# The norm's factor moved behind the rotation, in the first attention stage of a Perceiver block

## The reference

```python
def _rms_norm(t, w):                       # per head of 32 words
    var = jnp.mean(t * t, axis=-1, keepdims=True)
    return t * jax.lax.rsqrt(var + EPS) * w
def _rope(q, k, cos, sin):
    q1, q2 = jnp.split(q, 2, axis=-1); k1, k2 = jnp.split(k, 2, axis=-1)
    q_out = jnp.concatenate([q1 * cos - q2 * sin, q2 * cos + q1 * sin], axis=-1)
    k_out = jnp.concatenate([k1 * cos - k2 * sin, k2 * cos + k1 * sin], axis=-1)
    return (q_out, k_out)
q = _rms_norm(q, q_norm_w); k = _rms_norm(k, k_norm_w)
q, k = _rope(q, k, cos, sin)
attn = jnp.einsum('bhqd,bhkd->bhqk', q, k) * scale      # causal, softmax, times v, projection
```

## Time and profile before

| | us |
|---|---|
| Median of 3 runs (lowest, highest) | 2095.78 (2095.14, 2098.06) |
| The profiled execution: its own time | 2095.99 |
| Its span in the trace | 2094.4 |
| TensorE matmuls busy | 1946.4 (93%) |
| VectorE, ScalarE, GpSimd busy | 695.6, 542.0, 195.7 |
| The chain that ended last | TensorE 69%, issue 19%, GpSimd 4%, VectorE 4% |

### The profile page before, as it was taken

The page is one execution under the profiler, slowest core; times in us unless marked ns, Lnnn a source line. Parts: engine busy times, 40 slices in busy tenths (PEclk is TensorE's granted clock), DMA queues, the critical chain, the costliest instruction groups (busy, mean ns, idle before and its releaser), DMA issues.

```text
span 2094.4 us, 37583 instructions
## 1 busy us (share of the span) xinstructions
PE 1946.4 (93%) x15760; PEld 996.3 (48%) x15760; DVE 695.6 (33%) x1500; ACT 542.0 (26%) x1113; POOL 195.7 (9%) x182
## 2 busy tenths in 40 slices
PE   5888887999999999999997999999999999999976
PEld 2444464333333333333334656575666666565543
DVE  2666651122111211112122433334433333333322
ACT  1333211222222222222111233232323333232320
POOL 1122203000000000000003000000000000000000
PEclk8899998999999999999998999999999999999987
DMA  9544136999999999999975030000000100000000
GB/s 344 210 161 161 60 128 259 391 396 390 378 391 377 380 361 380 377 378 378 364 285 176 22 105 18 27 21 27 21 17 21 26 22 21 27 11 26 11 1 10
DMA packets 86296, 374.96 MB, mean 179 GB/s; under 512 B 7782, under 2 KB 25702, under 8 KB 53432
## 3 DMA queue, kind: packets, MB, share of 16 engines
q1 hardware_dynamic: 79544, 355.71, 44.5%
q0 software_dynamic: 6656, 17.77, 2.4%
HBM read 357.73 MB, written 16.45 MB: 179 GB/s over the span
## 4 chain that ended last, share of the span: by engine, by line
PE 69%; issue 19%; POOL 4%; DVE 4%; ACT 2%; DMA 1%; SPq 1%; another core or an unknown queue 0%; POOLq 0%; DVEq 0%; ACTq 0%
PE ps L1284 25%; PE ps L1462 16%; PE ps L1444 16%; POOL arena L540 4%; PE ps L1669 2%; PE ps L1452 2%; PE ps L1470 1%; DMA arena<-in_wproj0T 1%; PE ps L1590 1%; ACT arena L718 1%; PE ps L1344 1%; PE ps L1433 1%; PE ps L1374 1%; PE ps L1549 1%; PE ps L1611 1%
## 5 line engine op out<-in xcount | busy, mean ns | idle before, releaser
L1284 PE MATMUL ps<-arena 128*128 128x512 f32 (+3 forms) x3208 | 909.1, 440 | 26.1 <-ACT arena L661 8.5
L1284 PEld LDWEIGHTS ps<-arena 128*128 128x128 f32 x3208 | 548.0, 194 | 353.0 <-issue 291.2
L1462 PE MATMUL ps<-arena 128*32 128x512 f32 x3072 | 373.6, 594 | 0.0
L1444 PE MATMUL ps<-arena 128*32 128x512 f32 x3072 | 363.9, 596 | 0.7 <-issue 0.6
L540 POOL TENSOR_TENSOR arena<-arena 128x1 f32<-128x1 f32 (+3 forms) x80 | 128.3, 1604 | 1111.5 <-DVE arena L898 635.9
L1082 DVE COPY arena<-ps 128x512 f32<-128x512 f32 x96 | 66.4, 692 | 482.6 <-PE ps L1462 482.6
L1444 PEld LDWEIGHTS ps<-arena 128*32 128x32 f32 x3072 | 109.2, 109 | 226.0 <-issue 226.0
L1462 PEld LDWEIGHTS ps<-arena 128*32 128x32 f32 x3072 | 100.3, 109 | 198.2 <-issue 195.7
L768 ACT ACTIVATE arena<-ps 128x512 f32<-128x512 f32 x96 | 57.3, 597 | 353.0 <-PE ps L1444 353.0
L1181 DVE TENSOR_REDUCE arena<-ps 128x1 f32<-128x257 f32 x128 | 54.2, 424 | 154.7 <-PE ps L1549 152.6
L798 ACT ACTIVATE arena<-ps,arena 128x257 f32<-128x257 f32 x128 | 60.7, 477 | 141.4 <-PE ps L1284 141.4
(11 more groups left out here) (194 smaller groups left out, 1313.2 us busy)
## 6 DMA issues: line engine op xcount, KB each, us to landing
arena<-in_w SPq DMA_DIRECT2D x64, 4096.0 KB, 13.8
arena<-in_ctxT SPq DMA_DIRECT2D x8, 2056.0 KB, 7.9
arena<-in_ctxT SPq DMA_DIRECT2D x32, 514.0 KB, 3.7
arena<-in_ctx SPq DMA_DIRECT2D x8, 2048.0 KB
xe_rows<-arena SPq DMA_DIRECT2D x8, 616.0 KB
arena<-in_b POOLq DMA_DIRECT2D x32, 154.0 KB, 7.5
arena<-xe_rows SPq DMA_DIRECT2D x32, 154.0 KB
y_rows<-arena POOLq DMA_DIRECT2D x32, 154.0 KB, 6.2
```

The lines of the kernel that those rows point to most:

```text
L1284: ins = pe.matmul(dst, lhsT, rhs, start=(n == 0), stop=(n == len(pairs) - 1))
L1444: ins = pe.matmul(ps[q4[n], t, :], xeT[s][:, k, q4[t]], w1_sb[s][:, k, n * D:(n + 1) * D], start=(k == 0), stop=(k == KD - 1))
L1462: ins = pe.matmul(ps[q4[n], ST + t, :], hT[s][:, t, c, q4[n]], w2_sb[s][:, n * HB + c, :], start=(c == 0), stop=(c == HB - 1))
```

## The change

Before, the first of the five operations multiplies queries and keys (banks 4 and 5) by the factor `rs` and puts the result into SBUF (`qkn`); three multiplies by cosines and sines read it there, and an add gives `qkr`. After, the three multiplies read banks 4 and 5 directly, the add goes to `qkn`, VectorE waits for the factor only there, and a last operation multiplies `qkn` by it into `qkr`. The number and the sizes of the operations stay.

```diff
-                dve.wait_ge(rs_rdy, i + 1)
-                my.step(TT(qkn, ps[:, 4:6, :].rearrange("p a (h d) -> p (a h) d", h=H),
-                           bc(rs.unsqueeze(2), P, 2 * H, DH), ALU.mult))
                 v4 = "p (a h) d -> p a h d"
-                qn4, A4, B4 = (a.rearrange(v4, a=2) for a in (qkn, ropeA, ropeB))
+                A4, B4 = (a.rearrange(v4, a=2) for a in (ropeA, ropeB))
+                qn4 = ps[:, 4:6, :].rearrange("p a (h d) -> p a h d", h=H)
                 my.step(TT(A4, qn4, bc(CW.unsqueeze(2), P, 2, H, DH), ALU.mult))
                 hd = DH // 2
                 my.step(TT(B4[:, :, :, 0:hd], qn4[:, :, :, hd:DH],
                            bc(SW[:, :, 0:hd].unsqueeze(2), P, 2, H, hd), ALU.mult))
                 my.step(TT(B4[:, :, :, hd:DH], qn4[:, :, :, 0:hd],
                            bc(SW[:, :, hd:DH].unsqueeze(2), P, 2, H, hd), ALU.mult))
-                TT(qkr, ropeA, ropeB, ALU.add).then_inc(qkr_rdy, 1)
+                my.step(TT(qkn, ropeA, ropeB, ALU.add))
+                dve.wait_ge(rs_rdy, i + 1)
+                TT(qkr, qkn, bc(rs.unsqueeze(2), P, 2 * H, DH), ALU.mult).then_inc(qkr_rdy, 1)
```

## The result

| | before | after |
|---|---|---|
| Median of 10 runs, us (lowest, highest) | 2097.18 (2095.14, 2098.83) | 2091.61 (2087.61, 2092.11) |
| The profiled execution: its own time; its span | 2095.99; 2094.4 | 2089.46; 2087.9 |

The ratio is 0.9971 with a 95% interval of 0.9961 to 0.9981: 5.6 us faster, clear of noise. All of it arises in the first stage: from the issue of the first expert's weights (296.8 us before, 290.5 after) to the end it is 1797.6 and 1797.4 us.

A forecast was written before the change was run, and what follows sets the result against it. TensorE, busy for 93% of the span, was taken as the bound. Round 1 losing 0.5 us, rounds 2 to 6 gaining 0.5, round 7 1.8 and the clock 0.8 gave -2.6: 2093.4, as median 2093.2, range 2089.0 to 2097.2.

The forecast's parts named there:

- the likelier case: Whole kernel: a time within about 0.2%, 4.2 us, of no change, chance 0.67; faster 0.27, slower 0.06.
- The change on VectorE: Rotation out of PSUM: operations take 1.23 us, half ones 0.69; in round 2 VectorE is done 2.55 us earlier.
- Middle rounds: Rounds 2 to 6: line 1367 starts 0.1 us sooner in each, 0.5 us gained in all (0 to 0.9).
- Round 0 and round 1: Round 0 gains 3.6 to 7.1 us, all hidden by round 1's context transfer with its own date; 0.5 us lost.
- Round 7: Line 1367 no longer waits for VectorE: 1.8 us gained, 4.0 if the projection ran warm.
- The clock in the middle rounds: Falls of the clock after the idle stretch cost 1.6 us each; half a fall fewer, 0.8 us gained.
- Rival (a): Luck of the clock: two or more falls fewer, 2090.8 us, down to 2087.6 with none left; chance 0.21.
- The shared port: Rounds 0, 1, 7: the add might stand until the root's end, 259.8 in round 7; the sum stays.
- Rival (d): Rotation and root slow each other until they run one behind the other: 2095.5 us; chance 0.08.
- rival (b): Round 0's gain comes through if round 1's loads don't hold it: 3.6 to 7.1 us more, 2086 to 2090; chance 0.06.
- Rival (c): Slower: round 1 cold from line 1328 through line 1344 and the projection, rounds 2 and 5 fall too: 2100.5 us; 0.06.
- The signs: Trace of after: last of five operations waits for root, line 1367 never for VectorE, round 1's line 1344 at 77.4 or later.

The follow-up runs named there:

- e3: New order in round 0 alone, old order in the other rounds, against the kernel before: 2095.43 us, ratio 0.9994.
- e6: Changed kernel with the clearing of the experts' rows moved behind tile 2's context loads: 2085.56 us, ratio 0.9945 to the kernel before.
- e4: The whole change run again, beside the same runs of the kernel before as the partial ones: 2091.08 us, ratio 0.9969.
- e1: New order in round 7 alone, old order in rounds 0 to 6, against the kernel before: 2094.1 beside 2096.99 us, ratio 0.9987.
- e12: Kernel before (old order) with ten idle transposes a round and the clearing moved behind tile 2's context loads: 2084.68 us, ratio 0.9943.
- e11: Changed kernel with ten idle transposes a round and the clearing moved behind tile 2's context loads: 2077.94 us, ratio 0.9909 to the kernel before.
- e10: Kernel before (old order) with ten idle transposes behind line 1367 in each round: 2086.93 beside 2097.36 us, ratio 0.9953.
- e7: Changed kernel with ten idle transposes ahead of line 1374's wait in each round: 2081.79 us beside 2097.46 for the kernel before, ratio 0.993.
- e2: New order in rounds 2 to 6 alone, old order elsewhere, against the kernel before: 2094.59 us, ratio 0.9986.
- e5: Kernel before (old order) with the clearing of the experts' rows moved behind tile 2's context loads: 2096.35 beside 2097.46 us, ratio 0.9996.
- e8: Kernel before (old order) with GpSimd making the 128x32 root twice in each round: 2146.92 us beside 2096.11.
- e9: Changed kernel with GpSimd making the root twice in each round: 2116.55 us, beside 2096.11 for the kernel before.

## Why the prediction was right, point by point

The forecast was 2093.2 and the measured median 2091.6, inside the range. Part of this closeness is luck: the forecast starts from the first median of before, 2095.78, and over ten runs that is 2097.18. The gain is 5.6 us where 2.6 were forecast. I had held a time within 0.2% for the likelier case, and it is 0.29%, faster. The reasons, in the order of the prediction:

**The change on VectorE** was right: 1.22 and 0.69 us for the operations out of PSUM, in runs of 16 words too; the last multiply 2.7 us ahead of line 1367 in round 2.

**Middle rounds**: the place was right, the size half. I took 0.1 us for a round, from the first matmul of line 1367. It is 0.2 us, just outside my bounds (0.9 for five rounds; 1.0 came). What I had left out is that all its weight loads now run ahead. The first four transposes, for which ScalarE waits, take 0.45 us in the chain that ended last, where they took 0.61 to 0.65 before.

**Round 0 and round 1**: round 0's 3.64 us came (3.8). The further gain by a clock that holds did not: line 1374 of round 0 still took 1.94 us. That the transfer takes the gain back in round 1 was right in kind (e3, e6); line 1344 at 78.09 lies within what I had worked out, and the cold line 1328 took 3.35 us, a little over my 3.23. What failed is the step that gave the transfer a fixed date, and with it the sentence that all of round 0 is hidden: in e4 line 1344 started at 75.19, which I had named as a sign of being wrong. The transfer landed at 72.4 in one trace of the changed kernel and at 69.8 in the next. In the three traces with the old order in round 0 and the old place of the clearing, line 1367 of round 1 starts at 84.57, 85.40 and 86.01; in the three with the new one at 84.49, 81.58 and 85.54. That is 1.5 us earlier on the mean, with 0.6 us of it from an earlier start-up, so I put the term at about 1 us gained instead of 0.5 lost, and three traces a side can't size it better than to a microsecond.

**Round 7**: 1.8 us forecast, 1.9 in e1, 2.1 between e12 and e11. The 4.0 us that I had named for a warm projection came too, in the kernels with the filling; first e10, then e7:

```profile
248.25 5.40 PE L1284 MATMUL ps<-arena 128*128 128x512 f32 x8 [0.71 <-ACT arena L729]
...
256.73 1.09 PE L1367 MATMUL ps<-arena 128*128 128x128 f32 x8 [3.08 <-DVE arena L953]
```

```profile
248.86 3.71 PE L1284 MATMUL ps<-arena 128*128 128x512 f32 x8 [0.71 <-ACT arena L729]
...
253.44 1.09 PE L1367 MATMUL ps<-arena 128*128 128x128 f32 x8 [0.87 <-DVE arena L953]
```

With the projection at 3.71 us the last multiply is late next, and line 1367 comes 24.60 us behind that of round 6, where it is 28.57 in e10: 4.0 us. What I missed stands behind round 7. From line 1367 of round 7 to the weights' issue it is 34.2 us in all four unfilled traces with the old order there (before, e2, e3, e5) and 32.7 in all four with the new one (after, e1, e4, e6). The windows of that stretch show why; first before, then after, columns as in the earlier trace rows:

```profile
266.20:271.44 5.24, 2.69 (x37) 1.91 (x37) 2.72 (x4) 1.23 (x2) 0.00 (x0) 0.53 0.01 2
271.44:282.15 10.71, 10.71 (x44) 9.03 (x48) 4.32 (x11) 0.39 (x1) 0.00 (x0) 0.75 0.01 2
```

```profile
261.39:266.09 4.70, 1.67 (x37) 1.24 (x37) 2.89 (x5) 1.23 (x2) 0.00 (x0) 1.00 0.01 2
266.09:275.88 9.79, 9.79 (x44) 8.12 (x48) 4.32 (x11) 0.39 (x1) 0.00 (x0) 0.83 0.01 2
```

Before, TensorE stood for 1.8 us ahead of line 1367 and then for 2.6 us ahead of line 1374, and the clock had fallen by line 1374: it and line 1294 took 2.7 us instead of 1.7, and the product behind them 10.7 instead of 9.8. After, the first of these idle stretches is gone and the fall comes later. e10 and e12 show that this is the clock and not the order: they have the old order, but with the filling that stretch takes 32.7 us too. That is 1.5 us which I had, if anywhere, under luck.

**The clock in the middle rounds**: I took half a fall fewer in the six stretches behind rounds 1 to 6, 0.8 us. The first five are the intervals between the starts of line 1367 in rounds 1 to 6. The kernels with the old order in the loop have 3, 3, 3 and 3 long ones (before, e1, e3, e5), those with the new order 2, 3, 3 and 4 (after, e4, e6, e2). The sixth, behind round 6, has a fall in all four with the old order and in after and e4, but none in e2 and e6. Its first 3 us, before and then e2, columns as in the earlier trace rows:

```profile
236.25:239.25 3.00, 3.00 (x35) 2.00 (x35) 2.02 (x6) 1.88 (x2) 0.55 (x1) 0.50 0.97 338
```

```profile
237.55:240.55 3.00, 3.00 (x37) 1.84 (x38) 2.08 (x4) 1.85 (x2) 0.00 (x0) 1.00 1.06 372
```

So it is 4, 4, 4 and 4 falls with the old order and 3, 4, 3 and 4 with the new one, half a fall fewer on the mean, as I took. Four traces a side that differ by one fall or none don't show that the order is the cause, and that the shorter longest idle piece is the reason was argued, not tested. Rival (a), two or more falls fewer, was not what happened, though its number, 2090.8, is the nearest. The total came out larger than forecast because three other terms were sized too small or left out:

| | forecast, us | shown, us |
|---|---|---|
| rounds 0 and 1 | +0.5 | about -1 |
| rounds 2 to 6, by the order | -0.5 | -1.0 |
| rounds 2 to 6, by the clock | -0.8 | -0.8 on the mean, 0 to -1.6 by trace |
| round 7, the wait | -1.8 | -1.9 to -2.1 |
| behind round 7, by the clock | 0 | -1.5 |
| sum | -2.6 | about -6.3 (medians: -5.6 and -5.9) |

In the first pair of traces alone, before and after, the same terms are -0.1, -1.0, -1.6, -2.1 and -1.5: -6.3 us, which is the whole difference at the weights' issue (296.8 and 290.5). The medians' 5.6 us have an interval of 4.0 to 8.2, so they don't contradict it.

**The shared port**: neither engine gave way. In round 7 the add, line 951 (two SBUF inputs), runs from 251.99 to 253.22, all of it inside the root's 249.08 to 254.51, and takes 1.23 us, as it does in the middle rounds; the root takes its 5.43 us. The rule of the Trainium skill (SBUF — State Buffer, section Who interferes with whom), by which the add would have stood until the root's end, is not borne out by this pair of instructions; the measurement decides. **Rival (d)** is out by the same rows, **rival (b)** came true only in part, and for a reason that I had not given, an early landing. **Rival (c)**: line 1328 of round 1 ran cold, its line 1344 did not (2.92 us).

**The signs**: the operation that waits for the root is the last of the five, and from the projection to line 1367 it is 3.55 us, as I had said. That line 1367 would wait for VectorE in no round did not come true: in round 0 it still waits 0.95 us, as my own working of that round had it (1.1 us).

## What to carry to other kernels

Where a factor commutes with the work behind it, put the wait for it last: what counts is how many operations stand between the late value and the engine that waits, and e8 and e9 give the price of a longer root as 5.4 and 1.6 us a round. Then ask for each round what is late next. In one round it was the projection, in another a transfer behind others on its queue that could wait, and moving that transfer ahead is worth some 6 us only once the first wait is gone. And where rounds of one loop come in two lengths, look at the granted clock too: ten idle transposes a round were worth some 10 us here, more than the change, though 3 to 4 us of that lie in later stages, for a reason that is open.

## What the runs showed of the hardware that I had not expected

The transfer behind the clearing has no fixed date: the same transposed load took 17.6 to 19.6 us from issue to landing in the five traces of after and e1 to e4, and was issued between 52.2 and 54.8 us. Transposes of an identity into an unread bank keep TensorE at its 2.4 GHz level: 28.40 us for each of five rounds where two to four of them took 30.0. And where TensorE's idle time grows, the clock can add to its price: 5.4 us more of waiting made the rounds of e8 5.4 to 6.9 us longer than those of before with a fall, at a granted clock of 0.87 to 0.88 instead of 0.94.
